# The last layer's output bias of a graph network, added by one-row products or copied into the banks by ScalarE

## The reference, cut to what matters

```
h = relu(layernorm(x))
agg = segment_sum(h[dst], src)
h = (1 + eps) * h + agg
h = relu(h @ W1.T + b1)        # 512x512
h = h @ W2.T + b2              # 512x512, b2 has 512 values, one per output column
out = (h - mean) * rsqrt(var + 1e-5) * gamma + beta     # over the columns of a row
x = x + out
```

## Time and profile before

| | |
|---|---|
| device time, three runs | 393.66, 393.89, 395.64 us (median 393.89) |
| profiled execution: span from its first to its last instruction | 394.1 us |
| profiled execution: its own time | not given apart; it is its span and what lies around it |
| PE busy | 374.8 us, 95% |
| DVE busy | 312.1 us, 79% |
| ACT busy | 171.6 us, 44% |
| mean granted TensorE clock | 0.992 |

### The profile page before, as it was taken

One profiled execution on the slowest core, in us unless ns is written; L12 is line 12 of the kernel. 1 busy time (PEld: TensorE's weight loads), 2 busy tenths in 40 slices (PEclk: granted clock), 3 DMA queues, 4 the chain that ended last, 5 costly groups with the idle time before them and its releaser, 6 DMA issues.

```text
span 394.1 us, 5108 instructions
## 1 busy us (share of the span) xinstructions
PE 374.8 (95%) x1786; PEld 282.2 (72%) x1786; DVE 312.1 (79%) x660; ACT 171.6 (44%) x287; POOL 4.2 (1%) x19
## 2 busy tenths in 40 slices
PE   2989999999999999999999999999999999999994
PEld 1545566666657888887678788887588878787773
DVE  5889999999848789897868976698875788388236
ACT  5664666563044234244559533262363530145410
POOL 4000000000000000000000000000000000000000
PEclk9999999999999999999999999999999999999988
DMA  7602444343135000068200512200600050000002
GB/s 238 250 1 69 152 154 141 105 153 112 52 112 183 1 2 0 2 215 315 111 2 1 172 43 101 114 0 0 211 4 0 2 180 33 2 0 0 2 12 94
DMA packets 16360, 32.92 MB, mean 84 GB/s; under 512 B 1360, under 2 KB 1488, under 8 KB 16336
## 3 DMA queue, kind: packets, MB, share of 16 engines
q1 hardware_dynamic: 15744, 32.25, 23.9%
q10 hardware_dynamic: 592, 0.36, 0.3%
HBM read 21.07 MB, written 1.05 MB: 56 GB/s over the span
## 4 chain that ended last, share of the span: by engine, by line
PE 77%; DVE 14%; ACT 4%; issue 2%; DMA 1%; DVEq 0%; ACTq 0%
PE acc L1395 11%; PE bank L1377 10%; PE bank L1480 7%; PE bank L1270 6%; PE bank L1271 6%; PE bank L1251 4%; PE acc L1251 4%; PE acc L1271 4%; PE acc L1270 4%; PE bank L1465 3%; PE acc L1451 3%; DVE big_rounded L652 2%; PE acc L1228 2%; PE bank L1228 2%; PE acc L1545 2%
## 5 line engine op out<-in xcount | busy, mean ns | idle before, releaser
L1395 PE MATMUL acc<-wide_rounded,c_rounded 128*126 128x512 f32 x200 | 59.5, 439 | 0.7 <-ACT acc L464 0.7
L1395 PEld LDWEIGHTS acc<-wide_rounded,c_rounded 128*126 128x126 f32 x200 | 36.9, 186 | 19.8 <-issue 13.0
L792 DVE TENSOR_SCALAR wide_rounded<-iota_f,picked 128x512 fp32r<-128x512 f32 x100 | 42.2, 480 | 1.5 <-issue 1.1
L483 ACT COPY z_sb<-acc 126x512 f32<-126x512 f32 x37 | 21.6, 585 | 42.0 <-PE acc L1395 33.3
L507 ACT ACTIVATE wide<-wide,low_col 128x512 f32<-128x512 f32 x32 | 21.3, 715 | 32.9 <-DVE low_col L905 32.8
L1480 PEld LDWEIGHTS bank<-v_sb,big 128*128 128x128 f32 x256 | 29.7, 192 | 4.7 <-issue 4.0
L625 DVE TENSOR_TENSOR wslot_rounded<-wslot,wide_rounded 128x512 fp32r<-128x512 f32 x24 | 16.2, 687 | 21.2 <-ACT wslot L377 21.2
L1480 PE MATMUL bank<-v_sb,big 128*128 128x65 f32 x256 | 31.6, 277 | 0.0
L798 DVE TENSOR_TENSOR c_rounded<-row_bc,wslot_rounded 128x1008 fp32r<-128x1008 bf16 x25 | 30.0, 1201 | 0.0
L1377 PE MATMUL bank<-t_sb,wslot 128*128 128x512 f32 x64 | 29.5, 594 | 0.5 <-ACT t_sb L459 0.5
L652 DVE TENSOR_TENSOR big_rounded<-big,big_rounded 128x1024 fp32r<-128x1024 f32 x24 | 29.1, 1221 | 0.5
(11 more groups left out here) (312 smaller groups left out, 769.6 us busy)
## 6 DMA issues: line engine op xcount, KB each, us to landing
big<-z_sb SPq DMA_DIRECT2D x36, 252.0 KB
big<-in_w SPq DMA_DIRECT2D x4, 2048.0 KB, 7.8
x_sb<-in_x SPq DMA_DIRECT2D x8, 256.0 KB, 4.6
big<-in_w_3t SPq DMA_DIRECT2D x2, 1024.0 KB, 6.7
row_bc<-in_rows SPq DMA_DIRECT2D x7, 256.0 KB, 6.4
wslot<-in_wq SPq DMA_DIRECT2D x1, 1024.0 KB, 8.9
wslot<-in_wk SPq DMA_DIRECT2D x1, 1024.0 KB, 10.7
wslot<-in_wv SPq DMA_DIRECT2D x1, 1024.0 KB, 12.8
```

Source lines behind the costliest of these rows:

```text
L483: nc.scalar.copy(stage[0:BROWS, b % STAGES, :], a).then_inc(S["staged"], 1)
L792: nc.vector.tensor_scalar(hot_ring[:, u, k, :], iota_f[:, :], picked[:, 0, s0 + k:s0 + k + 1], None, ALU.is_equal)
L1395: last = nc.tensor.matmul(to, st_ring[:, u, 2 * k + a, :, :].rearrange("p w k -> p (w k)"), hot_ring[:, u, k, :], start=False, stop=False, ...
```

## The change

The eight one-row products and the three small rows that VectorE made for them are gone. ScalarE copies `rowp("b2_3")`, full 128 by 512, into banks 0 to 3, each copy after VectorE's `rest_of("gin_in", ...)` has read that bank, and ahead of ScalarE's `gin_mid` work. `gin2` starts no accumulation of its own; its products add to what the copies wrote, after one wait for all four copies. `gin2` has `group=2`: the highs of its first two tiles come before the lows of the first.

```diff
--- before.py
+++ after.py
@@ -181,8 +181,6 @@
         held_e = wide
         rcnt_bc, dinv_bc = rcnt_sb[:, :], iota_f[:, :]
         bn_t = wide[:, NT:, :]
-        b2_rows = [k_t_r[0:1, 0, :], k_t_r[0:1, 1, :]]
-        one_row = k_t_r[0:1, 2, 0:P]
 
 
 
@@ -237,7 +235,7 @@
             "ff1_ready", "ff2_mm", "deg_mm", "deg_diag", "deg_parts", "deg_std", "third_added", "loop_steps", "c2_turned", "c2_ready",
             "agg1_mm", "lin1_mm", "bn_var", "bn_std", "bn_coef", "bn_ready", "back_mm", "y_ready",
             "agg2_mm", "agg2_ready", "gcn1_mm", "gcn1_ready", "gcn2_mm", "gcn2_ready", "agg2b_mm", "agg3_mm",
-            "agg3_ready", "gin1_mm", "gin1_ready", "gin2_mm", "b2_rows", "out_ready")}
+            "agg3_ready", "gin1_mm", "gin1_ready", "gin2_mm", "b2_seeded", "out_ready")}
 
 
         parts, made = {}, {"hi_scalar": 0, "lo_vector": 0}
@@ -593,6 +591,11 @@
             for t in range(NT):
                 act.wait_ge(S["agg3_mm"], t + 1)
                 hi_part("gin_in", t, spare_at, bank[t][:, :])
+            act.wait_ge(S["rows_in"], 16 * (len(ROWS) - 1))
+            _, _, lo_by, before_lo = parts["gin_in"]
+            for t in range(NT):
+                act.wait_ge(S[lo_by], before_lo + t + 1)
+                nc.scalar.copy(bank[t][:, :], rowp("b2_3")).then_inc(S["b2_seeded"], 1)
             for t in range(NT):
                 act.wait_ge(S["gin1_mm"], t + 1)
                 twice("gin_mid", t, wide_lo, wide_at, bank[4 + t][:, :], ACT.Relu, "gin1_ready", bias=colp("b1_3", t))
@@ -1164,11 +1167,6 @@
             settle()
             for t in range(NT):
                 rest_of("gin_in", t, bank[t][:, :], spare_at, z_at)
-            nc.vector.tensor_copy(b2_rows[0], rowp("b2_3")[0:1, :]).then_inc(S["b2_rows"], 1)
-            nc.vector.tensor_copy(one_row, ones[0:1, :]).then_inc(S["b2_rows"], 1)
-            dve.wait_ge(S["b2_rows"], 2)
-            nc.vector.tensor_tensor(b2_rows[1], rowp("b2_3")[0:1, :], b2_rows[0].bitcast(F32), ALU.subtract
-                                    ).then_inc(S["b2_rows"], 1)
             for t in range(NT):
                 split_lo("gin_mid", t, wide_lo, wide_at, ready=("gin1_ready", 0))
             for t in range(NT):
@@ -1234,7 +1232,7 @@
                                                 stop=(n == len(terms) - 1))
                     last.then_inc(S[done], 1)
 
-            def product_in_parts(banks, lhs, rhs, ready, done, group=1, weight_lo=None, second=None, started=False,
+            def product_in_parts(banks, lhs, rhs, ready, done, group=1, weight_lo=None, second=None, seeded=False,
                                  by_tile=0, free={}):
 
 
@@ -1248,8 +1246,8 @@
                     for k, (a, r) in enumerate(terms):
                         if ready and m == 0:
                             pe.wait_ge(*ready[k][0])
-                        nc.tensor.matmul(bank[banks[m]][:, :], tile(a[0], m), r[0], start=(k == 0 and not started),
-                                         stop=False)
+                        nc.tensor.matmul(bank[banks[m]][:, :], tile(a[0], m), r[0], start=(k == 0 and not seeded),
+                                         stop=False, skip_group_check=seeded)
 
                 for k, (a, r) in enumerate(terms if by_tile else ()):
                     pe.wait_ge(*ready[k][0])
@@ -1267,9 +1265,10 @@
                     for k, (a, r) in enumerate(terms):
                         if ready and m == 0:
                             pe.wait_ge(*ready[k][1])
-                        nc.tensor.matmul(bank[b][:, :], tile(a[0], m), r[1], start=False, stop=False)
+                        nc.tensor.matmul(bank[b][:, :], tile(a[0], m), r[1], start=False, stop=False,
+                                         skip_group_check=seeded)
                         last = nc.tensor.matmul(bank[b][:, :], tile(a[1], m), r[0], start=False,
-                                                stop=(k == len(terms) - 1))
+                                                stop=(k == len(terms) - 1), skip_group_check=seeded)
                     last.then_inc(S[done], 1)
 
             def keep_warm(b, n):
@@ -1612,11 +1611,9 @@
             w_3 = weight("w_3")
             product_in_parts(hi, w_3[:NT], halves(spare_at, z_at), reads("gin_in"), "gin1_mm",
                              group=NT, weight_lo="w_3_lo", by_tile=NT)
-            pe.wait_ge(S["b2_rows"], 3)
-            for b in lo:
-                nc.tensor.matmul(bank[b][:, :], one_row, b2_rows[0], start=True, stop=False)
-                nc.tensor.matmul(bank[b][:, :], one_row, b2_rows[1], start=False, stop=False)
-            product_in_parts(lo, halves(wide_at, wide_lo), w_3[NT:], reads("gin_mid"), "gin2_mm", started=True)
+            pe.wait_ge(S["b2_seeded"], NT)
+            product_in_parts(lo, halves(wide_at, wide_lo), w_3[NT:], reads("gin_mid"), "gin2_mm", group=2,
+                             seeded=True)
 
 
 def kernel(**inputs):
```

## The result

| | before | changed |
|---|---|---|
| five runs each, us | 393.66, 393.89, 393.94, 395.27, 395.64 | 392.00, 392.28, 392.28, 392.29, 392.54 |
| median | 393.94 | 392.28 |
| profiled execution: its time | | 392.54 |
| profiled execution: its span | 394.1 | 391.0 |

The ratio is 0.9945, 95% interval [0.9925, 0.9966]: faster by 0.55%, about what the means of the five runs give (394.48 to 392.28); the medians give 0.42%. The forecast was 392.2 us, with a range of 390.1 to 393.0.

A forecast was written before the change was run, and what follows sets the result against it. TensorE (PE) was taken as the bound, with VectorE becoming it in the tail. Without a clock fall, 1.88 - 0.19 = 1.69 us, so 393.89 - 1.7 = 392.2 us, range 390.1 to 393.0.

The forecast's parts named there:

- What bounds the kernel: Whole kernel: TensorE (PE), busy 95% of the span; time leaving its last-layer stream leaves the total unless another engine binds.
- The copies at nothing: ScalarE before gin_mid: four copies end between 365.8 and 366.3, at least 2.1 us before its next work; cost nothing.
- The one-row products, 1.88 us: Start of gin2: without them the fourth high, limited by ScalarE, moves from 376.64 to 374.76, 1.88 us earlier.
- the sum: Last layer: 1.88 + 1.78 - 0.19 = 3.47 us gain against an execution with the clock fall, 1.69 without.
- The order, 0.19: Tail: with group=2 the second tile follows after 1.82 us, VectorE becomes the bound, giving back 0.19 to 0.43; 0.19 taken.
- The clock, 1.78: Inside gin2: half clock cost 1.50 in the first tile plus 0.28 in the second, removed if tied to one-row products.
- Which group is the median: Runs before: the median 393.89 was read as without a clock fall, the profiled execution as with one; gain 1.7.
- The chances: Whole kernel, against a 0.5% threshold: faster 0.41, same 0.55, slower 0.04.
- The medians with the fall: Runs before: their median already included the clock fall, so the full 3.47 us shows, giving 390.4 us; chance 0.37.
- The fall that stays: gin2: half clock independent of one-row products remains, costing 1.78; result 392.2 to 392.5 or about 394.0; chance 0.09.
- The rule of the Trainium skill: gin2: clock drops after long PE idle; by it alone 1.78 us is not gained, profiled span 392.4 rather than 390.6.
- Slower through the pause: Fourth high of gin2: waiting for ScalarE lowers the clock for longer; two half-clock stretches give 395.8 us; chance 0.04.

The follow-up runs named there:

- sixteen copies: The changed kernel with twelve more 128x512 ScalarE copies, to idle SBUF, three ahead of each of the four into the banks: 393.06 us.
- the order by k: The changed kernel with by_tile=2: for each part of gin_mid, the first tile's high, then the second tile's; 391.50 us.
- the first set: First of three sets of follow-up runs, each on one chip, with the unchanged kernel timed alongside; 11 of its 29 runs there had the clock fall.
- the third set: Last of three sets of follow-up runs, on one chip: changed kernel again 392.06 us, its group=1 form 391.91, six highs ahead of the waiting one 391.65.

## Why the prediction was right

**What bounds the kernel.** Right. PE and then VectorE carry the last layer, and each microsecond taken from or added to the tail came out in the time: 1.12 in the tail and 1.13 in the time with sixteen copies, 0.16 and 0.15 for the order.

**The copies at nothing.** Right. They ended 2.95 us ahead of ScalarE's next work where 2.1 or more was forecast, and an experiment with twelve more showed when the cover ends.

**The one-row products, 1.88 us.** Right, and confirmed by two traces: from `gin1`'s last product to the first low of `gin2` it is 377.00 - 373.59 = 3.41 us before and 374.91 - 373.40 = 1.51 us with the copies and group=1, 1.90 less. The start 0.04 us behind ScalarE was as in the earlier trace rows. It put the fourth high at 375.10 - 0.34 = 374.76 on the clock of before, as forecast. What I passed over in the same rows is that the product there was recorded with 0.50 us, where an ordinary one has 0.39: a product behind a pause was slow. The three highs ahead of the pause end at 374.15 + 3 x 0.227 = 374.83, so PE waited 0.27 us, within the 0.1 to 0.3 that I named; but the five starts from 375.10 to the first low at 376.36 took 1.26 rather than 1.14, so that the order by k gained 0.38. It didn't spoil the sum because the highs behind the one-row products of before were slow as well (1.04 us for four rather than 0.91), which I had not seen either. That two oversights of 0.12 and 0.13 us cancel is luck.

**The order, 0.19.** Right: VectorE became the bound, at 2.47 us a tile, and 0.15 to 0.16 us was given back. The larger value, 0.43, assumed 2.56 a tile; the overlap read from the earlier trace rows decided it.

**The clock, 1.78.** That the fall goes with the one-row products is shown; the size was too large. The two groups of the kernel before have medians of 393.68 and 395.31 in the first set, 1.63 apart. The term that was mis-sized is the 1.50 for the first tile: I compared its 4.22 us with 2.72, but with four one-row products ahead and no fall that tile took 2.89. So 1.33 + 0.28 = 1.61. With the measured terms the tail moves by 1.90 + 1.61 - 0.16 = 3.35 us, which is 15.23 - 11.88; the sum had 3.47. On the clock of before PE's last product starts at 384.88 (forecast 384.7) and the last statistics at 385.47 (385.3 to 385.6). For the same reason the span forecast of 390.6 for an execution like the profiled one was a little low: its own span is 391.0, and the five were 390.5 to 391.0.

**Which group is the median.** Right, on the argument used: three runs split 2 to 1 by the price of the fall, and a profiled span above the median. The 1.5 us around a span, seen only now, and the spans and clocks of the later runs settle it. The forecast of 1.7 us was taken against the lower group: 393.89 (median of its three runs among the first five) - 392.28 = 1.61, or in the third set 393.60 (median of the six lower runs) - 392.06 = 1.54. The forecast time, 392.2, rests on this reading and came out at 392.28 and, in the third set, at 392.06.

**The chances.** By the ratio the change lies just beyond the bound of 0.5%, on the side to which I gave 0.41, and by the medians (0.42%, forecast 0.43%) just within it, on the side to which I gave 0.55. The difference between the two is the falls, which a mean feels and a median of five with two falls does not. How large the change looks depends on the share of falls in the runs of before: with 8 of 14 in the upper group its median is 395.25, and the same changed kernel is at 0.9935. So the time of the changed kernel was worked out, but how large the change looks was in part luck: at 24 of 64 a median of five runs of before would be one with a fall about once in four times (an estimate from that share).

**The rivals.** The medians with the fall: excluded for the first five runs, though it describes the third set. The fall that stays: 0 of 11 runs of the changed kernel, 0 of 23 with full-height products, and 0 of 40 in the six other runs of kernels with the copies, so excluded as far as 74 runs can. The rule of the Trainium skill weighed for it (TensorE: Matmul & The Clock Gate, "Why this matters for your kernels"), that the clock drops behind a long gap with PE idle, does not explain this fall: it came with PE recorded busy (3.30 of 3.30 us ahead of it), and with full-height products in the same place it did not come. Slower through the pause: the pause was there, 0.27 us long, and the clock stayed at 1.00.

## What to carry to other kernels

Read the granted clock next to what the engine did before it changed, and count a group of one-row products as a risk to the products behind it: here eight in a row cost 1.9 us always and 1.6 us more in 24 of 64 runs. A seed by an engine that is idle takes both away, if its copies end before that engine's next work; a full-height form of the same products takes away the second and 0.4 us of the first. When products are reordered to fill a wait, work out the spacing of the tiles that come out, not only the end of the product: two tiles 1.8 us apart in front of an engine that needs 2.47 give back part of the gain.

## What the runs showed of the hardware that was not expected

- The clock fell to half while PE was recorded busy throughout, behind 8 one-row products in some executions and behind 16 in all; with the same products at full height in none (0 of 23), and behind 4 one-row products in none (0 of 9).
- Going from 128-row products to one-row ones and back cost about 0.4 us beyond their number: 393.68 against 393.28 us.
- A pause of 0.27 us on PE cost 0.38: eight highs took 2.21 us in place of 1.83, since the first product behind the pause was slow too (about 0.34 us to the next start instead of 0.23).
- Copies of 128x512 on ScalarE follow one another at 0.52 us although each is recorded with 0.58 to 0.62.
